# Causal attention on one core: the mask moves from a TensorE product into VectorE's row reduction, and neighbouring row tiles share one reciprocal

## The reference

```
K, Q, V = xn W_K, xn W_Q, xn W_V           # 16 heads of 64
scores  = Q K^T, entries with key > query set to -1e10
attn    = softmax(scores / 8)              # over the keys
z       = attn V
out     = z W_O                            # summed over the heads
moe     = 9 experts (128 -> 352 -> 128, silu gate), the top 2 of a softmax router
```

## Time and profile before

| | |
|---|---|
| median of 3 runs | 704.05 us (703.42 to 705.62) |
| span of the profiled execution, first to last instruction | 699.8 us |
| what the median has beyond that span | 4.2 us |
| PE busy | 675.4 us, 97% of the span |
| PEld busy | 596.0 us, 85% |
| DVE busy | 612.5 us, 88% |
| ACT busy | 543.2 us, 78% |
| POOL busy | 487.2 us, 70% |
| share of the chain that ended last | PE 73%, DVE 4%, ACT 1%, POOL 1% |
| granted TensorE clock, mean | 0.990 |

### The profile page before, as it was taken

How to read it: one execution, slowest core, us unless ns; L and a number is a source line. 1 busy time by engine, 2 the same in 40 slices (tenths; PEclk the granted TensorE clock), 3 DMA queues, 4 the chain that set the end, 5 groups by cost and what they waited for, 6 DMA issues and landing times.

```text
span 699.8 us, 14966 instructions
## 1 busy us (share of the span) xinstructions
PE 675.4 (97%) x4845; PEld 596.0 (85%) x4845; DVE 612.5 (88%) x1401; ACT 543.2 (78%) x1280; POOL 487.2 (70%) x494
## 2 busy tenths in 40 slices
PE   7879999989999999999999999999999999999996
PEld 6669999868888898988888989888888888887886
DVE  8977777778989899999999999999999999898986
ACT  5745555578888898988888888888888888888873
POOL 5374344166788786878786868687968686979861
PEclk9789999999999999999999999999999999999999
DMA  7614622125253333333342514252516151616001
GB/s 236 181 30 117 167 74 60 37 53 126 49 125 77 87 88 80 79 85 85 90 100 63 124 43 115 48 122 54 140 27 140 28 139 25 141 28 157 6 26 35
DMA packets 50235, 61.03 MB, mean 87 GB/s; under 512 B 7440, under 2 KB 28272, under 8 KB 50160
## 3 DMA queue, kind: packets, MB, share of 16 engines
q1 hardware_dynamic: 47856, 55.36, 32.8%
q0 software_dynamic: 2304, 4.72, 2.9%
HBM read 12.87 MB, written 4.72 MB: 25 GB/s over the span
## 4 chain that ended last, share of the span: by engine, by line
PE 73%; DVE 4%; ACT 1%; POOL 1%; issue 1%; ACTq 0%
PE ps_big L1382 20%; PE ps_mid L1417 17%; PE ps_z L1438 7%; PE ps_z L1437 7%; PE ps_misc L1245 5%; PE ps_misc L1247 4%; PE ps_misc L1246 4%; PE ps_big L1438 3%; PE ps_big L1437 3%; PE ps_big L1379 2%; DVE pT_lo L1151 1%; DVE neg_max L1105 1%; ACT pT_hi L860 0%; DVE z_sum L1159 0%; PE ps_misc L1253 0%
## 5 line engine op out<-in xcount | busy, mean ns | idle before, releaser
L687 POOL TENSOR_TENSOR probs<-probs,rden 128x1024 f32<-128x1024 f32 (+7 forms) x256 | 295.2, 1166 | 108.7 <-DVE rden L1140 105.8
L860 ACT ACTIVATE pT_hi<-ps_mid 128x512 fp32r<-128x512 f32 (+3 forms) x384 | 184.4, 493 | 66.4 <-PE ps_mid L1417 63.0
L1151 DVE TENSOR_TENSOR pT_lo<-ps_mid,pT_hi 128x512 fp32r<-128x512 f32 (+3 forms) x384 | 206.8, 549 | 11.6 <-ACT pT_hi L860 7.9
L1382 PE MATMUL ps_big<-k_st,q_st 128*128 128x512 f32 (+2 forms) x768 | 213.9, 382 | 0.0
L1105 DVE TENSOR_REDUCE neg_max<-ps_big 128x1 f32<-128x1024 f32 (+7 forms) x256 | 192.6, 752 | 21.6 <-PE ps_big L1382 18.2
L847 ACT ACTIVATE probs<-ps_big,neg_max 128x1024 f32<-128x1024 f32 (+7 forms) x256 | 190.1, 743 | 5.2 <-DVE neg_max L1105 3.2
L1417 PE MATMUL ps_mid<-ident,probs 128*128 128x128 f32 x1152 | 177.5, 273 | 4.9 <-DVE pT_lo L1151 4.3
L1417 PEld LDWEIGHTS ps_mid<-ident,probs 128*128 128x128 f32 x1152 | 134.3, 140 | 19.2 <-issue 11.8
L1382 PEld LDWEIGHTS ps_big<-k_st,q_st 128*128 128x128 f32 x768 | 117.7, 194 | 1.8
L1437 PE MATMUL ps_z<-pT_hi,v_st 128*128 128x256 f32 x448 | 116.5, 290 | 0.0
L1438 PE MATMUL ps_z<-pT_lo,v_st 128*128 128x256 f32 x448 | 112.7, 282 | 0.0
(11 more groups left out here) (243 smaller groups left out, 1249.4 us busy)
## 6 DMA issues: line engine op xcount, KB each, us to landing
k_st<-k_st SPq DMA_DIRECT2D x90, 256.0 KB
q_st<-q_parts SPq DMA_DIRECT2D x128, 128.0 KB
y_dram<-y_sb SPq DMA_DIRECT2D x40, 64.0 KB
k_st<-k_parts SPq DMA_DIRECT2D x8, 256.0 KB
raw_gu<-in_L_ffn_Wg_dram SPq DMA_DIRECT2D x9, 176.0 KB, 3.0
raw_gu<-in_L_ffn_Wu_dram SPq DMA_DIRECT2D x9, 176.0 KB, 3.2
raw_d<-in_L_ffn_Wd_dram SPq DMA_DIRECT2D x9, 128.0 KB, 3.1
res<-in_L_attn_x_dram SPq DMA_DIRECT2D x4, 256.0 KB, 3.8
```

The costliest lines, as they stand in the source:

```text
L687: pool.tensor_tensor(rows, rows, col.to_broadcast([P, width]), ALU.mult).then_inc(normed, 1)
L860: nc.scalar.activation(pT_hi[:, t:t + 2 * tiles - 1:2, :], ps_mid[:, bank, 0:tiles * P].rearrange("p (t q) -> p t q", t=tiles), ACT.Copy). ...
L1151: nc.vector.tensor_tensor(pT_lo[:, at, :], ps_mid[:, bank, 0:tiles * P].rearrange("p (t q) -> p t q", t=tiles), pT_hi[:, at, :].bitcast(F3 ...
L1382: ins = nc.tensor.matmul(ps_big[:, n % 2, c0:c1], w, k_st[half][h][:, part, c0 - off:c1 - off], start=part == 0 and not masked, stop=part ...
```

## The change

1. The mask product of TensorE is gone, and with it `causal_bf`. A constant `later` in SBUF (128x1024, bf16) holds +1e30 in its last 128 columns where the key is later than the query, and 0 elsewhere. GpSimd makes it during the expert stage.
2. The queries' weights are scaled by -1/8 in place of 1/8, so the scores come out negated.
3. `row_max` is a fused operation, `tensor_tensor_reduce`: it adds `later` to the negated scores, writes the sum back to the same PSUM columns, and gives the minimum as its accumulator output. That minimum is the negated row maximum. ScalarE takes `exp(-1 * column + minimum)`.
4. `recip` is called for odd units only, and makes the reciprocals of units n-1 and n in one instruction of two columns. In `DVE_ORDER` all steps `R` with an even number go; the others stay where they were. GpSimd's `norm` of unit n waits for the reciprocal with the number n // 2 + 1.

```diff
-            Cq0 L14.0- X3 L14.1- R1 L15.0- R2 X4 Cq1 L0.0 L0.1 R3 X5 L1.0 R4 Z2- X6 L2.0 L2.1 X7 R5 Ck1 R6 L3.0
...
+            Cq0 L14.0- X3 L14.1- R1 L15.0- X4 Cq1 L0.0 L0.1 R3 X5 L1.0 Z2- X6 L2.0 L2.1 X7 R5 Ck1 L3.0
...
-                pool.wait_ge(rden_done, unit_count(p, n))
+                pool.wait_ge(rden_done, UPH * p + n // 2 + 1)
                 pool.tensor_tensor(rows, rows, col.to_broadcast([P, width]), ALU.mult).then_inc(normed, 1)
...
-                    nc.scalar.activation(w_hi[:, 0, :], bank[:, 0:P], ACT.Copy, scale=DH ** -0.5)
+                    nc.scalar.activation(w_hi[:, 0, :], bank[:, 0:P], ACT.Copy, scale=-DH ** -0.5)
...
-                                     bias=neg_max[:, n:n + 1], accum_out=den[:, n:n + 1]).then_inc(exp_done, 1)
+                                     bias=neg_max[:, n:n + 1], scale=-1.0, accum_out=den[:, n:n + 1]).then_inc(exp_done, 1)
...
-                nc.vector.tensor_reduce(neg_max[:, n:n + 1], ps_big[:, n % 2, off:off + width], AX_X, ALU.max,
-                                        negate=True).then_inc(max_done, 1)
+                cols = ps_big[:, n % 2, off:off + width]
+                nc.vector.tensor_tensor_reduce(cols, cols, later[:, S - width:S], 1.0, FLOOR, ALU.add, ALU.min,
+                                               neg_max[:, n:n + 1]).then_inc(max_done, 1)
...
                 if n == SUBS:
+                    dve.wait_ge(later_made, 1)
                     row_max(0, 0)
...
-                nc.vector.reciprocal(rden[:, n:n + 1], den[:, n:n + 1]).then_inc(rden_done, 1)
+                nc.vector.reciprocal(rden[:, n - 1:n + 1], den[:, n - 1:n + 1]).then_inc(rden_done, 1)
...
-                    masked = c0 <= diag < c1
-                    if masked:
-                        nc.tensor.matmul(ps_big[:, n % 2, diag:diag + P], ident_bf[:], causal_bf[:],
-                                         start=True, stop=False, skip_group_check=True)
```

More of the change, by code:

```diff
@@ L17 @@
 MASKED = -1e30
+FLOOR = 3e38
 def bass_layernorm_causal_attention_plus_moe_kernel(
@@ L96, in bass_layernorm_causal_attention_plus_moe_kernel @@
         ident_bf = sb("ident_bf", [P, P], BF16)
-        causal_bf = sb("causal_bf", [P, P], BF16)
         eps_col = sb("eps_col", [P, 1])
@@ L219, in bass_layernorm_causal_attention_plus_moe_kernel @@
         wo_twice = sb("wo_twice", [P, 2, 2, D], F32R)
+        later = sb("later", [P, S], BF16)
         x_in = [sem(f"x_in{g}") for g in range(TB)]; xn_out = sem("xn_out")
@@ L225, in bass_layernorm_causal_attention_plus_moe_kernel @@
         out_sent = sem("out_sent")
-        acc_zero = sem("acc_zero"); voted = sem("voted"); counted = sem("counted")
+        acc_zero = sem("acc_zero"); later_zero = sem("later_zero"); later_made = sem("later_made"); voted = sem("voted"); counted = sem("counted")
         sub_ready = sem("sub_ready"); sub_scaled = sem("sub_scaled"); row_ready = sem("row_ready")
@@ L312, in bass_layernorm_causal_attention_plus_moe_kernel @@
         DVE_ORDER = read("""
-            Cq0 L14.0- X3 L14.1- R1 L15.0- R2 X4 Cq1 L0.0 L0.1 R3 X5 L1.0 R4 Z2- X6 L2.0 L2.1 X7 R5 Ck1 R6 L3.0
-            Cv0 X8 L4.0 L4.1 R7 Cv2 X9 Z3- R8 L5.0 Cv3 X10 L6.0 Co1- X11 R9 L6.1 L7.0 Cv1 X12 R10 L8.0 R11 Co0-
-            L8.1 R12 X13 L9.0 Cwo X14 R13 Cwqkv+ L10.0 L10.1 X15 Z0 R14 Ck0+ L11.0 X0+ R15 L12.0 X1+ L12.1 Z1
-            L13.0 X2+ R0+""")
+            Cq0 L14.0- X3 L14.1- R1 L15.0- X4 Cq1 L0.0 L0.1 R3 X5 L1.0 Z2- X6 L2.0 L2.1 X7 R5 Ck1 L3.0
+            Cv0 X8 L4.0 L4.1 R7 Cv2 X9 Z3- L5.0 Cv3 X10 L6.0 Co1- X11 R9 L6.1 L7.0 Cv1 X12 L8.0 R11 Co0-
+            L8.1 X13 L9.0 Cwo X14 R13 Cwqkv+ L10.0 L10.1 X15 Z0 Ck0+ L11.0 X0+ R15 L12.0 X1+ L12.1 Z1
+            L13.0 X2+""")
         POOL_ORDER = read("""
@@ L593, in _ @@
             pool.memset(ident_bf[:], 0.0).then_inc(pool_order, 1)
-            pool.memset(causal_bf[:], 0.0).then_inc(pool_order, 1)
             pool.memset(before_bf[:], 0.0).then_inc(pool_order, 1)
@@ L597, in _ @@
             pool.memset(eps_col[:], EPS).then_inc(const_made, 1)
-            pool.wait_ge(pool_order, 5)
+            pool.wait_ge(pool_order, 4)
             pool.affine_select(out=ident[:], in_=ident[:], compare_op=ALU.not_equal, fill=1.0, base=0,
@@ L601, in _ @@
             pool.affine_select(out=ident_bf[:], in_=ident_bf[:], compare_op=ALU.not_equal, fill=1.0, base=0,
-                               pattern=[[-1, P]], channel_multiplier=1).then_inc(const_made, 1)
-            pool.affine_select(out=causal_bf[:], in_=causal_bf[:], compare_op=ALU.is_ge, fill=MASKED, base=0,
                                pattern=[[-1, P]], channel_multiplier=1).then_inc(const_made, 1)
@@ L650, in _ @@
             pool.memset(acc[:], 0.0).then_inc(acc_zero, 1)
+            pool.wait_ge(wlo_dve, len(DVE_LO))
+            pool.memset(later[:], 0.0).then_inc(later_zero, 1)
+            pool.wait_ge(later_zero, 1)
+            pool.affine_select(out=later[:, S - P:S], in_=later[:, S - P:S], compare_op=ALU.is_ge, fill=-MASKED, base=0,
+                               pattern=[[-1, P]], channel_multiplier=1).then_inc(later_made, 1)
             pool.wait_ge(down_done, SUBS)
@@ L942, in split_proj @@
                 if name == "wqkv":
-                    nc.vector.scalar_tensor_tensor(out=w_lo[:, 0, :], in0=bank[:, 0:P], scalar=DH ** -0.5,
+                    nc.vector.scalar_tensor_tensor(out=w_lo[:, 0, :], in0=bank[:, 0:P], scalar=-DH ** -0.5,
                                                    in1=w_hi[:, 0, :].bitcast(F32), op0=ALU.mult, op1=ALU.subtract)
@@ L1006, in _ @@
             dve.wait_ge(shifted, 1)
-            dve.wait_ge(const_made, 10)
+            dve.wait_ge(const_made, 9)
             now = logit
@@ L1373, in scores @@
                 off, width, parts = score_cols(i)
-                diag = off + width - P
                 w = q_st[half][h][:, i * P:(i + 1) * P]
                 for c0, c1 in parts:
-                    masked = c0 <= diag < c1
-                    if masked:
-                        nc.tensor.matmul(ps_big[:, n % 2, diag:diag + P], ident_bf[:], causal_bf[:],
-                                         start=True, stop=False, skip_group_check=True)
                     for part in range(2):
                         ins = nc.tensor.matmul(ps_big[:, n % 2, c0:c1], w, k_st[half][h][:, part, c0 - off:c1 - off],
-                                               start=part == 0 and not masked, stop=part == 1, skip_group_check=True)
+                                               start=part == 0, stop=part == 1, skip_group_check=True)
                 ins.then_inc(s_ready, 1)
```

## The result

| | before | after |
|---|---|---|
| median | 703.84 us (4 runs, 703.42 to 705.62) | 814.28 us (4 runs, 813.68 to 814.44) |
| span of the profiled execution | 699.8 us | 812.6 us |
| ratio | | 1.156, 95% interval 1.153 to 1.158 |

The change makes the kernel 15.6% slower, 110.4 us. 808 us were predicted, with 760 to 845 us as the range.

What follows compares the result with a forecast made beforehand. TensorE was taken as the bound. Stalls 7.3 plus reads 0.35 less masks 0.8 gave 6.85 us a half, 110 for 16, less 5; with 699.8 span and 4.2 overhead 809, written 808 us, range 760 to 845.

Steps and rivals of the forecast that it cites:

- `T0` waits: TensorE's transposes of unit 0 wait for its normalisation, delayed to unit 1's reciprocal: 1.8 us late.
- `T2` waits: TensorE's transposes of unit 2 wait for its normalisation, delayed to unit 3's reciprocal: 1.2 us late.
- `T4` waits: TensorE's transposes of unit 4 wait for its normalisation, delayed to unit 5's reciprocal: 2.2 us, the largest.
- `T6` waits: TensorE's transposes of unit 6 wait for its normalisation, delayed to unit 7's reciprocal: 1.2 us without value projections.
- `Mo1` waits: TensorE's output product waits for `Z1` on GpSimd, late behind unit 6's normalisation: another 0.9 us.
- `T8` waits: TensorE's transposes of unit 8 wait for its normalisation, delayed to unit 9's reciprocal: 1.0 us without value projections.
- Rival (a): TensorE's stalls: only the large delays count, others are absorbed; 743 us, or 778 with two more pairs; chance 0.13.
- The accumulator read: New reads on VectorE, 0.07 us each, some 5 times a half in the delayed chains: +0.35 us.
- rival (b): TensorE's clock falls at the longest stall of each half: 56 us more, 865 us; chance 0.05.
- The mask's own gain: Mask products leaving TensorE's queue save 1.6 us in a half, 26 us in all, if nothing waits.
- Rival (d): TensorE stays the bound and the whole 26 us of the masks comes: faster, 678 us; chance 0.05.
- Rival (c): VectorE's fused operation passes one column in two cycles, 9.8 us more a half, making VectorE the bound: 880 us; chance 0.05.

Runs made afterwards that it cites:

- the shared reciprocals alone: Kernel before with the even reciprocals dropped as in the change, mask product and plain reduction kept: 825.79 us, ratio 1.173.
- the first pair alone: Fused mask as in the change, with only the reciprocals of units 0 and 1 shared, all others as before: 719.52 us, ratio 1.021.
- the pair 4 and 5 shared: Fused mask as in the change, with only the reciprocals of units 4 and 5 shared: 728.92 us, ratio 1.034.
- the mask part: Kernel after with the old `DVE_ORDER` and one reciprocal per unit, so only the fused mask differs from the kernel before: 691.74 us, ratio 0.982.
- the kernel without the mask product: Kernel before with TensorE's mask product dropped and nothing in its place: 689.86 us, ratio 0.979.
- six shared early: Kernel after with odd reciprocals moved forward in VectorE's order, and units 4 and 6 given reciprocals of their own: 689.83 us, ratio 0.978.

## Why the prediction was right

The prediction's steps, against what the traces show:

| step | predicted, us | measured, us |
|---|---|---|
| `T0` waits | 1.8 | 1.80 |
| `T2` waits | 1.2 | 1.10 |
| `T4` waits, half without / with value projections | 2.2 / 1.5 | 2.30 / 1.61 |
| `T6` waits | 1.2 / 0 | 1.12 / none |
| `Mo1` waits | 0.9 | 1.17 / 1.02 |
| `T8` waits | 1.0 / 0.3 | 0.94 / none |
| `T12` waits | 0.3 | 0.26 |
| all waits of a half, mean | 7.3 | 7.25 (8.7 and 5.8) |
| what the masks still give | 0.8 | 0.7 (from 825.8 - 814.3) |
| a half longer by | 6.85 | 7.0 |

- *The chain.* The cause is the one named: the normalisation of an even, wide unit starts at the reciprocal of the next unit, and TensorE meets the transposes before it is done. The experiments show each link: the shared reciprocals alone make the slowdown, one pair alone costs its stall, and moving them forward without unsharing them takes most of it back.
- *That the delays add* was argued from where each reciprocal stands. The trace has each at its own full size in one half, and the first pair alone costs 1.74 us in a half. Rival (a) is out. TensorE was foretold near 85% busy in a steady window; it is busy for 80.9 us from 200 to 300, 84.6 from 300 to 400 and 80.8 from 560 to 660.
- *The accumulator read* was priced at 0.07 us. It moves the next start by 0.00 us. The 0.35 us of it in the chains was not there. That the sum came out even so has another reason: the waits less the masks are 7.25 - 0.7 = 6.6 us, and a half is longer by 6.94 us on average, since a stall costs 0.1 us or more beyond its idle row (seven of them in a half without value projections). The sum had no such term. That the two are of one size is luck.
- *The clock, rival (b),* was right in kind and small in size: not each half, but four times in the attention of the kernel after, where stretches of 40 us show a clock of 0.96 in place of 1.00. My stalls, which I had thought short enough, stand in front of all four: 2.04 us (to 155.5), 2.30 (to 365.7), 2.30 (to 406.9) and 1.82 (to 479.4). But little of it reaches the time. The three halves that can be set against the same kind of half with a full clock are 0.2, 0.4 and 0.6 us longer, as `T6` (or, behind the last, `T2`) then does not wait. That is 1 to 2 us in all, where rival (b) had 56.
- *The mask's own gain* was the weakest term. Each mask costs the 0.12 us that I read, but the 26 us, "if nothing waits", were too much: without any shared reciprocal only 12 to 14 us come. TensorE at 99.64 us of 100 looked like the only bound, and yet two fifths of what was taken out of its queue came back (0.95 us of 1.6 arrive in a half). Which waits took it is shown only for the rows above. Rival (d) had been priced by that number, and 678 us was out of reach for this change in any order of its reciprocals that I tried.
- *Terms that offset each other.* The halves were forecast at 105 us after 5 us off for the first one. From the first `N0` on they bring 108: the first and the last are shorter by 4 us together than the mean, so the 5 were of the right size, but stand for both ends. Another 4.6 us are lost ahead of the first `N0`, which no term of the sum has; they are in the last section. And I added 4.2 us for what the median has beyond the span. The later kernels have 1.8 us there (814.44 us of the profiled execution against its 812.6), so the profiled execution of the kernel before was itself a quick one, by some 2.4 us, and the 4.2 were not all overhead.

## What to carry to other kernels

An instruction of 0.07 us, dropped once in each of 16 halves, cost 28 us here, because it releases another engine: before two small operations are merged, read how long the earlier one's consumer takes, where the consumer's consumer stands, and how much room there is between them. If merged, put the merged one where its last input is ready, not where the second one used to stand. And a busy share of 99% is no promise that work taken away comes back in full: ask which waits stand just behind it. Last, a local loss is not yet a loss of time: before a slow stretch is priced, set its half against one without it.

## What had not been expected of the hardware

- The read of the accumulator on VectorE has a row of 138 ns on average and took none of its sequence: at 309.98 and at 311.52 the next instruction starts with it, and the fused operation with its read is 1.01 us from start to start for 896 columns, as the plain reduction was. It read PSUM and bf16 in SBUF and wrote back to the same PSUM columns at the pace of the plain reduction, 1228 ns for 1024 columns against 1225. Rival (c) is out. (Its 9.8 us for the 9216 columns of a half would be 11.0 by nine times the 1225 ns it names, so it would have been dearer still.)
- Stalls of 2.2 to 2.3 us were followed by the lower clock in some halves and not in others: seven of nine with the pair 4 and 5 shared, two of nine in the kernel after. Those of 1.8 us were too, but rarely: once in the kernel after (479.4), and once with the first pair shared, in the last half (window 677:682 above, behind 1.81 us). What decides between them stays open.
- At the start the clock differs between these traces: 0.94 up to 20 us in the kernel before, 0.80 in the mask part. In that trace the first normalisation of 1024 columns starts at 149.04 us against 144.52, and in the kernel without the mask product, where the clock was 0.86, at 147.96. The runs speak for chance rather than for the change. One and the same kernel has both: the kernel before goes from a clock of 0.990 and a span of 699.6 us to 0.981 and 704.0 to 705.3, and that with six shared early has four runs at 0.982 to 0.984 (687.4 to 689.4 us) and two at 0.989 (685.1 us). The profiled execution of the kernel before, with 0.990, is one of its quickest, while the kernel after stood at 0.976 to 0.978 in all four runs, some 0.984 without its four slow stretches in the attention (an estimate: four times 40 us at 0.96 in 812.6). So of the 4.6 us between the first `N0` before and after, some or all may be the execution that was profiled. What sets the clock at the start stays open; a longer warm-up did not change it.
